# Splitting the waits of three-part products: rounded halves first, remainders last, and one projection issued earlier

## The reference

```
x = x + 0.5 * ffn(layernorm(x))      # 1792 hidden channels, each weight is w * (su @ sv), rank 4
x = x + attention(layernorm(x))      # 32 query heads, 8 key/value heads of 128, causal, ALiBi bias
x = x + 0.5 * ffn(layernorm(x))      # the same weights again
ffn(t)  = down(silu(gate(t)) * up(t))
attention: q, k = rmsnorm per head; softmax(q k^T / sqrt(128) + bias) v; then Wo
```

## Time and profile before

| what | value |
|---|---|
| median of the runs | 1282.38 us |
| profiled execution, its own time | 1279.44 us |
| span of that execution | 1278.1 us |
| busy: PE, weight loads, DVE, ACT, POOL | 1243.2, 1058.0, 809.6, 732.9, 526.2 us |
| PE busy in 285 to 1008 us (slots 1 to 59) | 721.99 of 723.00 us |
| PE busy in 0 to 101, 1008 to 1052, 1052 to 1090 us | 81.91 of 101, 38.38 of 44, 34.34 of 38 us |
| granted PE clock | 1.00 |

### The profile page before, as it was taken

One profiled execution on the slowest core, in us unless ns is written; L12 is line 12 of the kernel. 1 busy time (PEld: TensorE's weight loads), 2 busy tenths in 40 slices (PEclk: granted clock), 3 DMA queues, 4 the chain that ended last, 5 costly groups with the idle time before them and its releaser, 6 DMA issues.

```text
span 1278.1 us, 18363 instructions
## 1 busy us (share of the span) xinstructions
PE 1243.2 (97%) x6562; PEld 1058.0 (83%) x6562; DVE 809.6 (63%) x1978; ACT 732.9 (57%) x1738; POOL 526.2 (41%) x412
## 2 busy tenths in 40 slices
PE   5999999999999999999999999999999989999999
PEld 4777888788888888888888888888888777788887
DVE  7866666675656666566566566666656767655555
ACT  3544443257657667667666667667667674444442
POOL 5586551634224324315315314313413344575550
PEclk9999999999999999999999999999999999999999
DMA  6043222101001001001101001001001010121101
GB/s 224 36 139 118 102 101 99 51 1 50 34 1 50 34 1 50 34 1 50 34 1 50 34 1 51 34 1 50 34 1 50 11 40 1 51 69 64 50 17 66
DMA packets 15018, 60.20 MB, mean 47 GB/s; under 512 B 2064, under 2 KB 2736, under 8 KB 12880
## 3 DMA queue, kind: packets, MB, share of 16 engines
q1 hardware_dynamic: 14544, 58.47, 13.0%
q10 hardware_dynamic: 384, 0.56, 0.1%
HBM read 45.91 MB, written 13.11 MB: 46 GB/s over the span
## 4 chain that ended last, share of the span: by engine, by line
PE 90%; DVE 4%; ACT 2%; issue 2%; POOL 1%; DMA 1%; SPq 0%; DVEq 0%; ACTq 0%
PE bank L284 27%; PE bank L285 27%; PE bank L286 27%; PE bank L479 5%; PE bank L458 2%; PE bank L312 1%; DVE mix_l L1024 1%; PE bank L461 1%; DVE mix L1015 1%; ACT prob L790 0%; ACT prob L799 0%; DVE probT_l L1169 0%; DVE raw_early L926 0%; DMA x_rows<-x 0%; POOL w_l_early L1254 0%
## 5 line engine op out<-in xcount | busy, mean ns | idle before, releaser
L1332 POOL TENSOR_TENSOR rows<-rows,row_root_y 128x640 f32<-128x640 f32 x64 | 80.6, 1259 | 272.0 <-DVE row_root_y L892 272.0
L790 ACT ACTIVATE prob<-prob,neg_top 128x128 f32<-128x128 f32 (+3 forms) x256 | 141.0, 552 | 75.8 <-DVE neg_top L1158 75.2
L1326 POOL TENSOR_TENSOR square<-rows 128x640 f32<-128x640 f32 x64 | 80.3, 1254 | 205.5 <-ACT rows L769 205.5
L805 ACT CAST probT_h<-bank 128x512 fp32r<-128x512 f32 x160 | 84.5, 596 | 136.9 <-PE bank L479 136.9
L799 ACT ACTIVATE prob<-prob,inverse 128x128 f32<-128x128 f32 (+3 forms) x256 | 122.9, 554 | 1.8 <-DVE inverse L1163 1.8
L284 PE MATMUL bank<-w_h_late,xnT_hi 128*128 128x512 f32 (+1 forms) x352 | 121.2, 344 | 0.0
L286 PE MATMUL bank<-w_h_late,xnT_lo 128*128 128x512 f32 (+1 forms) x352 | 118.6, 337 | 0.0
L285 PE MATMUL bank<-w_l_late,xnT_hi 128*128 128x512 f32 (+1 forms) x352 | 118.3, 336 | 0.0
L1254 POOL TENSOR_TENSOR w_l_late<-raw_late,w_h_late 128x512 fp32r<-128x512 f32 (+1 forms) x58 | 88.5, 1545 | 69.4 <-ACT w_h_late L585 69.4
L1169 DVE TENSOR_TENSOR probT_l<-bank,probT_h 128x512 fp32r<-128x512 f32 x160 | 101.6, 685 | 21.9 <-ACT probT_h L805 21.7
L1183 DVE TENSOR_TENSOR x_rows<-bank,x_rows 128x512 f32<-128x512 f32 x64 | 44.2, 690 | 105.0 <-PE bank L286 105.0
(11 more groups left out here) (175 smaller groups left out, 3510.3 us busy)
## 6 DMA issues: line engine op xcount, KB each, us to landing
raw_late<-w_qkv SPq DMA_DIRECT2D x8, 1536.0 KB, 6.3
raw_early<-ffn_w SPq DMA_DIRECT2D x21, 512.0 KB, 3.8
scaled<-raw_early SPq DMA_DIRECT2D x21, 512.0 KB, 2.6
raw_late<-scaled SPq DMA_DIRECT2D x21, 512.0 KB, 3.6
raw_late<-w_o SPq DMA_DIRECT2D x8, 1024.0 KB, 4.8
y<-x_rows SPq DMA_DIRECT2D x8, 256.0 KB, 2.0
x_rows<-x SPq DMA_DIRECT2D x6, 256.0 KB, 5.2
x_rows<-x ACTq DMA_DIRECT2D x2, 256.0 KB, 4.3
```

Of the source, the lines that this page charges most:

```text
L790: last = act.activation(p, p, ACT.Exp, bias=neg_top[:, h:h + 1], scale=-1.0, accum_out=total[:, h:h + 1])
L805: act.copy(probT_h[:, j, :, :], banks[r.bank][:, :].rearrange("p (h q) -> p h q", h=G)).then_inc(probT_hi_done, 1)
L1326: pool.tensor_tensor(square[:, n % 2, :, :], row, row, ALU.mult).then_inc(squares_done, 1)
L1332: pool.tensor_tensor(row, row, by, ALU.mult).then_inc(rows_normed, 1)
```

## The change

`first_gate_up` takes the place of the first call of `gate_up` (line 527). It issues 8 matmuls of rounded with rounded parts for both halves, then 8 with the rests of the tokens, then 8 with the rests of the weights, and waits ahead of each third for what it needs.

`down`, `weigh_values` and `project_out` no longer use matmul3. They issue all matmuls on the rounded part of the fresh operand (two for each chunk) after a wait for `..._hi_done`, and then those on its rest (one for each chunk) after the wait that stood in front of everything. The number of matmuls and their operands are the same.

The q part of the projection of unit 4 moves from slot 0, where it stood behind the scores of unit 0, to the end of `from_ffn_to_attention`, ahead of these scores. ScalarE's copy of that result stays where it was, in ScalarE's slot 0.

```diff
--- before.py
+++ after.py
@@ -327,19 +327,46 @@
                                        k == 0, k == KC - 1)
                     last.then_inc(full[r.bank], 1)
 
+            def first_gate_up(p):
+
+                _, w_h, w_l = room[p]
+                two = [result("gate_up", p, 0, 0, 0, half) for half in range(2)]
+                pe.wait_ge(ffn_hi, split_nth(p, 0, "a12") + 1)
+                pe.wait_ge(xn_hi, xn_nth(2 * p, 0, TB - 1) + 1)
+                for part, (w_part, t_part) in enumerate(((w_h, xnT_hi), (w_h, xnT_lo), (w_l, xnT_hi))):
+                    if part == 1:
+                        turned = results["xn", 2 * p, 0, TB - 1]
+                        pe.wait_ge(evac[turned.bank], turned.nth)
+                    if part == 2:
+                        pe.wait_ge(ffn_lo, split_nth(p, 0, "a12") + 1)
+                    for half, (r, bank) in enumerate(two):
+                        for k in range(KC):
+                            w = START["gu0"] + (2 * k + half) * P
+                            last = pe.matmul(bank[:, :], w_part[:, w:w + P], t_part[:, k, 0:S],
+                                             start=part == 0 and k == 0, stop=part == 2 and k == KC - 1)
+                        if part == 2:
+                            last.then_inc(full[r.bank], 1)
+
             def down(p, s, b, blocks=range(TB)):
                 _, w_h, w_l = room[p]
                 _, _, d_hi, d_lo = gated[p]
                 pe.wait_ge(ffn_lo, split_nth(p, s, "d1") + 1)
-                pe.wait_ge(d_done, max(gate_nth(p, s, c, b) for c in range(CH)) + 1)
                 for t in blocks:
                     r, bank = result("down", p, s, b, t)
                     tokens = slice(t * P, (t + 1) * P)
+
+                    for nth, c in enumerate(sorted(range(CH), key=lambda c: gate_nth(p, s, c, b))):
+                        w = START["down"] + c * DM
+                        w = slice(w, w + DM)
+                        if t == blocks[0]:
+                            pe.wait_ge(d_hi_done, gate_nth(p, s, c, b) + 1)
+                        pe.matmul(bank[:, :], d_hi[:, c, b, tokens], w_h[:, w], start=nth == 0, stop=False)
+                        pe.matmul(bank[:, :], d_hi[:, c, b, tokens], w_l[:, w], start=False, stop=False)
+                    if t == blocks[0]:
+                        pe.wait_ge(d_done, max(gate_nth(p, s, c, b) for c in range(CH)) + 1)
                     for c in range(CH):
                         w = START["down"] + c * DM
-                        w = slice(w, w + DM)
-                        last = matmul3(bank[:, :], (d_hi[:, c, b, tokens], d_lo[:, c, b, tokens]), (w_h[:, w], w_l[:, w]),
-                                       c == 0, c == CH - 1)
+                        last = pe.matmul(bank[:, :], d_lo[:, c, b, tokens], w_h[:, w:w + DM], start=False, stop=c == CH - 1)
                     last.then_inc(full[r.bank], 1)
 
             def product(p, s, m):
@@ -434,6 +461,7 @@
                         turn_normed(1, 1, (0, 1))
                 turn_rows(0)
                 turn_normed(1, 1, (2, 3))
+                project(LEAD, "q")
 
             def project(n, part):
                 g, b, t = unit(n)
@@ -484,30 +512,37 @@
                 values = results["kv", n]
                 pe.wait_ge(evac[values.bank], values.nth)
                 r, bank = result("values", n)
+                turned = [p_part[:, j, :, :].rearrange("p h q -> p (h q)") for j in range(i + 1) for p_part in (probT_h, probT_l)]
                 for j in range(i + 1):
-                    turned = results["turn_prob", n, j]
-                    pe.wait_ge(evac[turned.bank], turned.nth)
-                    last = matmul3(bank[:, :], (v_h[:, b, j, :], v_l[:, b, j, :]),
-                                   (probT_h[:, j, :, :].rearrange("p h q -> p (h q)"), probT_l[:, j, :, :].rearrange("p h q -> p (h q)")),
-                                   j == 0, j == i)
+                    pe.wait_ge(probT_hi_done, probT_nth(n, j) + 1)
+                    pe.matmul(bank[:, :], v_h[:, b, j, :], turned[2 * j], start=j == 0, stop=False)
+                    pe.matmul(bank[:, :], v_l[:, b, j, :], turned[2 * j], start=False, stop=False)
+                for j in range(i + 1):
+                    r_turned = results["turn_prob", n, j]
+                    pe.wait_ge(evac[r_turned.bank], r_turned.nth)
+                    last = pe.matmul(bank[:, :], v_h[:, b, j, :], turned[2 * j + 1], start=False, stop=j == i)
                 last.then_inc(full[r.bank], 1)
 
             def project_out(n):
                 g = unit(n)[0]
                 weighed = results["values", n]
-                pe.wait_ge(evac[weighed.bank], weighed.nth)
                 r, bank = result("out", n)
+                pe.wait_ge(oT_hi_done, n + 1)
                 for h in range(G):
                     if n % (B * TB) == 0:
                         pe.wait_ge(o_lo, g * G + h + 1)
-                    last = matmul3(bank[:, :], (oT_h[:, h, :], oT_l[:, h, :]), (o_h[:, h, :], o_l[:, h, :]), h == 0, h == G - 1)
+                    pe.matmul(bank[:, :], oT_h[:, h, :], o_h[:, h, :], start=h == 0, stop=False)
+                    pe.matmul(bank[:, :], oT_h[:, h, :], o_l[:, h, :], start=False, stop=False)
+                pe.wait_ge(evac[weighed.bank], weighed.nth)
+                for h in range(G):
+                    last = pe.matmul(bank[:, :], oT_l[:, h, :], o_h[:, h, :], start=False, stop=h == G - 1)
                 last.then_inc(full[r.bank], 1)
 
             def slot(n):
                 scores(n)
                 if n:
                     weigh_values(n - 1)
-                if n + LEAD < UNITS:
+                if n and n + LEAD < UNITS:
                     project(n + LEAD, "q")
                 if n + 1 < UNITS:
                     turn_rows(n + 1)
@@ -524,7 +559,7 @@
             turn_normed(0, 0)
             scale_weights(0, "gu1")
             scale_weights(0, "down")
-            gate_up(0, 0, 0, 0)
+            first_gate_up(0)
             ffn_first(0)
             ffn_second(0)
             for s in range(2, STEPS - 1):
```

## The result

The changed kernel takes 1283.59 us (median, 1282.15 to 1285.37, 22 runs) where the kernel before, on the same chip, takes 1281.32 (1279.42 to 1283.15, 22 runs). The ratio is 1.002, with a 95% interval from 1.0013 to 1.0026: the change costs 2.3 us. That is clear of the noise of these runs, and just under the 0.2% that was to count as a difference. The profiled execution has a span of 1281.2 us (own time 1282.52); that of before had 1278.1 and 1279.44.

A forecast was written before the change was run, and what follows sets the result against it. TensorE, busy 97% of the span, was taken as the bound, so only its idle time could be won. Terms 0.3 + 4.8 - 2.2 + 1.3 - 2.1 + 0 + 0 - 0.8 = +1.3 on 1282.38 gave 1283.7 us, range 1282.0 to 1285.4.

The forecast's parts named there:

- project_out, +4.8: First unit of seven groups: six matmuls instead of three behind the last o_lo wait, 0.69 us each, +4.8 us in all.
- Rival 1: Faster: no o_lo term in project_out, because the rests are in time for the new order; 1278.9 us, chance 0.22.
- weigh_values, -2.2: Units with one block of keys: the 0.31 us stall for probT_l goes; seven slots count, -2.2 us.
- The moved projection, +1.3: Before slot 0: twelve matmuls push the first scores by 1.8 us, about 0.5 hidden; cost +1.3 us.
- `down`, -2.1: Four rounded matmuls of the first block cover at most 0.92 us of each d_lo wait; four places, -2.1 us in all.
- first_gate_up, 0: First gate_up call: TensorE starts up to 1.2 us earlier, but the following `down` hangs on VectorE's d_lo; 0 us.
- the tail, 0: Units 60 to 62: oT_l waits shrink, but TensorE then waits for the next softmax; 0 us, other end -3.2.
- The last weigh_values: Last unit's weigh_values: one matmul instead of twelve after the last rest's arrival, ending 1051.0 instead of 1051.87; -0.8 us.
- Rival 3: The tail's oT_l waits in project_out are won in full, 3.2 us; 1280.5 us, no measurable change, chance 0.06.
- Met waits, +0.3: 282 added waits on TensorE's stream, already met when reached, cost 1 ns each; +0.3 us.
- Rival 2: Slower: added waits cost 10 ns each even when met, in all 64 slots; 2.8 us, 1286.2 us, chance 0.19.
- rival 4: A met wait on TensorE exposes the weight load, 0.1 us for each of 282, 28 us; 1312 us, chance 0.03.

The follow-up runs named there:

- the two kernels with the old first order: Changed kernel with project_out of each group's first unit in its old order: 1277.88 us; the same with the moved projection also back in its place: 1277.54 us.
- the kernel without the o_l stall: Changed kernel with each group's first project_out issuing the rests of o last: 1275.42 us; the same without the moved projection: 1274.20 us.
- the two other orders of project_out: Changed kernel with each group's first project_out in the old order, 1277.88 us, or with the rests of o last, 1275.42 us; without the move 1277.54 and 1274.20.

## Why the forecast was right, and what it lacked

The forecast of 1283.7 us lies 0.1 beside the measured 1283.59, and that is in part luck: it stood on 1282.38 for the kernel before, which took 1281.32 in this series, and the change cost 2.3 instead of 1.3. What can be judged are the terms of the sum. Stage by stage and without the fall of the clock they come to +1.2, where +1.3 was forecast.

**project_out, +4.8.** Held. Seven groups, 0.69 each when the old order is put back, eight in the kernel with this edit alone. The forecast had the whole stall ahead of part 3; it is spread over parts 2 and 3, 0.32 and 0.77 us. The first group was taken as 0, with the other end at +0.7, because slot 0 lets the rest run ahead. That reason is right for most of it: without the move that group pays 0.68, and with it only the 0.24 shown above. The net 0 (slot 1 took 10.78 and takes 10.73) needs besides the 0.3 that slot 1 wins elsewhere, which the forecast did not count. Rival 1, the absent o_l term, is out.

**weigh_values, -2.2.** Held: 0.29 in seven slots is 2.0, and the slots at the start of a group gave nothing, since the wait for o_l is absolute.

**The moved projection, +1.3.** The pieces were right, the size somewhat too large. Scores of unit 0 come 1.5 to 1.7 later (1.8 forecast; 1.67 between the two kernels with the old first order), and slot 0 gives back 0.53 (0.5). The 0.3 more that slot 1 gives back in the kernel with the move alone was not in the sum. The term is 0.66 alone, 1.2 in the kernel without the o_l stall, and 0.5 where it also takes most of that stall off the first group. Both waits of slot 0 came as described.

**`down`, -2.1.** -1.91 of it in the first pass; measured -1.95 with `down` alone, -1.91 in the changed kernel once the 1.67 of the move is taken out (-0.91 + 0.67 - 1.67). The -0.17 of `down`(1, 0, 0) is not seen: without a fall of the clock, that last stretch takes 210.7 to 210.9 us with either order. The product behind it waits for w_l_late, which comes when GpSimd brings it, and what `down` wins is 0.8 more of that wait.

**first_gate_up, 0, and the tail, 0.** The first held; the experiment with first_gate_up alone shows the won 1.4 us waited for ahead of `down`. In the tail, three waits for oT_l (3.2) became three for oT_h (1.8), and qT_l took over 0.9 of them: slots 60 to 62 are 0.26 shorter. The last weigh_values and the tail together are -0.80, as was forecast; the 0.26 was not in the sum. Rival 3, which had all 3.2 won, is out.

**Met waits, +0.3.** They cost nothing measurable. Rival 2 and rival 4 are out. What the Trainium skill says in "TensorE: Matmul & The Clock Gate", section "Step-by-step: what each phase is for", on weight loads that are pulled ahead of running matmuls, goes together with this: 336 waits put ahead of matmuls left slots 2 to 59 at 713.55 us against 713.59, so as far as the time tells, a met wait does not stop it.

**What was missing** is the clock. The sum of stages without the fall is +1.2, the medians of all runs differ by 2.3, and at equal clocks by 2.1 and 1.1. The mean number of falls, one for 0.999, two for 0.997, three for 0.996, is (8 + 2 x 12) / 23 = 1.4 for before and (9 + 2 x 6 + 3 x 7) / 22 = 1.9 for the changed kernel. At 1.3 to 1.6 us each, half a fall more is an estimate of 0.7 to 0.8 us, most of the 1.1 that are left. (No profile was taken at 0.996; its three falls are an extension of the series.) The move seems to make a place for one, behind its two waits in slot 0: two of five profiles with it have a fall there, none of nine without it. That it is also why the changed kernel has falls in every run is open: taking it out moved the clocks of that kernel (0.996 in 7 of 22 runs to none in 11, 1.000 in none to six), but not those of the kernels with the two other orders of project_out.

## What to carry over

Splitting a product into rounded and rest parts helps only for the operand whose rest is late; look at every operand of the product, and put last the part that depends on the latest of them. What a late operand costs is the number of matmuls behind its wait times their spacing, so that reordering that is free elsewhere is a loss in the one unit where the other operand's rest is late. At a wait that hangs on another engine's queue, time won earlier is not won.

## What the runs showed of the hardware

- The clock falls to its lower level (0.50, 1.2 GHz) for some 3.4 us in some executions and not in others of the same program. The 14 profiled executions hold 17 falls. Eleven stand behind two waits less than 4 us apart: 1.26 and 0.78 us at 35 us, 1.06 and 0.95 in slot 0, 1.65 and 2.25 near 1090 us, but also 0.84 and 2.25. One stands behind 3.28 and 1.96 us, over 6 us apart. Five stand behind a single wait of 1.88 to 2.42 us, as in the kernel with the new `down` alone, at the weigh_values of the last unit, whose matmuls start 0.57 and 0.42 us apart from the first on:

```profile
1047.54 0.77 PE L284 MATMUL bank<-probT_h,v_h 128*128 128x512 f32 x1 [2.31 <-DVE probT_l L1176]
1048.11 0.63 PE L285 MATMUL bank<-probT_l,v_h 128*128 128x512 f32 x1
1048.53 0.63 PE L286 MATMUL bank<-probT_h,v_l 128*128 128x512 f32 x1
```

  The profiled execution of before has waits of 1.89 us at 35 us, 2.30 at 1049 and 0.84 and 2.25 near 1089, and no fall. So such waits alone do not decide it. Most falls cost 1.3 to 1.7 us, 0.1% of this kernel, as much as an edit is worth. With differences of this size, the mean clocks of the runs belong beside their medians. The Trainium skill, "TensorE: Matmul & The Clock Gate", section "What's actually happening", says that the gate watches TensorE's activity on a time base of its own, which no kernel's start resets, so that the same program changes its clock at different points from run to run. The spread of levels agrees with it; no run here shows the time base.
- A fall need not cost what it takes from TensorE. The kernel with the met waits had one at 21 to 24 us, and its stretch from the first matmul to the scaling of the weights was 37.16 us against 36.67, 0.5 longer instead of some 1.6. The wait ahead of `down`(0, 0, 0), which hangs on VectorE's d_lo, took up the rest; it was 1.89 us before:

```profile
36.06 0.47 PE L284 MATMUL bank<-w_h_early,d_hi 128*128 128x512 f32 x1 [0.53 <-issue]
```

  The next stretch of that execution was 1.3 shorter than before (229.59 against 230.87), nearly all of it in one wait at 100 us, for raw_early, of 0.39 instead of 1.61 us; its cause is open. Falls in cheap and in costly places would also make two groups of times at one mean clock, as the runs of before at 0.999 have them; that is argued, not shown.
- 336 waits on semaphores long since reached had no price on TensorE's stream (713.55 us against 713.59). A matmul behind a wait that did block is followed 0.08 to 0.11 us late (0.31 to 0.34 us after its start instead of 0.23).
